# Attention and mixing decoder on one core: the transposed scores six steps behind the row maxima in place of eight

## What is computed

```python
x = x + _L0_attn_ref(_layernorm(x), w_qkv, w_proj)
# in it, for each of 16 sequences b and 16 heads h:
attn = jnp.einsum('bnhd,bmhd->bhnm', q, k) * SCALE
attn = jax.nn.softmax(jnp.where(causal, attn, NEG), axis=-1)
out = jnp.einsum('bhnm,bmhd->bnhd', attn, v)      # then a bit-linear projection
# in the feed-forward network, for gate_w, up_w and down_w:
wq = w.astype(jnp.float8_e4m3fn).astype(x.dtype)
```

## Time and profile before

| | us |
|---|---|
| median of 3 runs (1488.34 to 1490.43) | 1490.22 |
| the profiled execution | 1488.82 |
| its span, first to last instruction | 1487.0 |
| PE, DVE, ACT, POOL busy, of the span | 1390.5, 1234.5, 871.8, 1177.6 |
| time outside the span, in the profiled execution | 1.8 |
| first row scores begin | 48.83 |
| first transposed scores begin | 76.26 |
| attention steady, eight steps | 24.79 |
| last maxima of rows begin | 442.41 |

### The profile page before, as it was taken

The page is one execution under the profiler, slowest core; times in us unless marked ns, Lnnn a source line. Parts: engine busy times, 40 slices in busy tenths (PEclk is TensorE's granted clock), DMA queues, the critical chain, the costliest instruction groups (busy, mean ns, idle before and its releaser), DMA issues.

```text
span 1487.0 us, 23871 instructions
## 1 busy us (share of the span) xinstructions
PE 1390.5 (94%) x8327; PEld 775.5 (52%) x8405; DVE 1234.5 (83%) x1964; ACT 871.8 (59%) x1437; POOL 1177.6 (79%) x902
## 2 busy tenths in 40 slices
PE   3698999999986898899999999999999999999998
PEld 2577787878764443334444444444444444444443
DVE  6789999999984799789898899899889888888611
ACT  5589999999886223444545455455456446544341
POOL 3279999999985687888888878878887888788532
PEclk9799999999998899999999999999999999999999
DMA  5545565655431533222422331332323232240001
GB/s 191 132 111 152 139 167 139 167 139 152 127 83 58 175 100 81 68 50 71 100 50 52 91 78 43 79 78 64 78 64 71 62 81 50 68 102 15 18 19 29
DMA packets 171587, 133.57 MB, mean 90 GB/s; under 512 B 120500, under 2 KB 124748, under 8 KB 171468
## 3 DMA queue, kind: packets, MB, share of 16 engines
q1 hardware_dynamic: 171276, 131.91, 35.4%
q10 hardware_dynamic: 192, 0.14, 0.0%
HBM read 50.67 MB, written 19.92 MB: 47 GB/s over the span
## 4 chain that ended last, share of the span: by engine, by line
PE 64%; DVE 12%; POOL 8%; issue 7%; ACT 7%; DMA 1%; SPq 0%; POOLq 0%; DVEq 0%; ACTq 0%
PE gu L839 20%; PE gu L853 10%; PE shared_bank L784 9%; POOL pL L1782 3%; PE y L806 3%; PE y L800 3%; PE y L803 3%; PE y L808 3%; PE y L809 3%; DVE blockmax L980 2%; DVE o_sb L1020 2%; DVE z L1210 1%; DVE qkt L960 1%; PE s_kq L632 1%; ACT pH L1427 1%
## 5 line engine op out<-in xcount | busy, mean ns | idle before, releaser
L1654 ACT ACTIVATE shared<-shared_bank 128x512 f32<-128x512 f32 x162 | 96.1, 593 | 320.5 <-PE shared_bank L784 320.5
L1207 DVE TENSOR_TENSOR y<-shared,y 128x512 f32<-128x512 f32 x324 | 223.9, 691 | 41.2 <-ACT shared L1654 22.1
L1782 POOL TENSOR_TENSOR pL<-pT,pH 128x768 f16<-128x768 f32 x128 | 217.0, 1698 | 12.9 <-ACT pH L1427 7.4
L839 PE MATMUL gu<-fT,wg 128*128 128x512 f16 x768 | 181.4, 379 | 1.5 <-DMA fT<-fnl 1.5
L1214 DVE TENSOR_REDUCE oT<-z 128x64 f32<-128x512 f32 x256 | 175.6, 686 | 8.7
L839 PE MATMUL gu<-fT,wu 128*128 128x512 f16 x768 | 182.2, 380 | 0.0
L1210 DVE TENSOR_TENSOR z<-y,cT 128x512 f32<-128x512 f32 x236 | 162.3, 688 | 10.7 <-PE y L798 4.4
L1916 POOL TENSOR_TENSOR fuL<-fu,fuH 128x512 f16<-128x512 f32 x96 | 112.0, 1167 | 71.8 <-ACT fuH L1669 71.6
L853 PE MATMUL gu<-wd,fuL 128*128 128x512 f16 x384 | 145.6, 379 | 0.0
L853 PE MATMUL gu<-wd,fuH 128*128 128x512 f16 x384 | 145.6, 379 | 0.0
L1852 POOL TENSOR_TENSOR kv<-vT,cT 128x1024 f32<-128x1024 f32 x70 | 137.8, 1970 | 5.9 <-ACT vT L1609 5.9
(11 more groups left out here) (222 smaller groups left out, 3540.2 us busy)
## 6 DMA issues: line engine op xcount, KB each, us to landing
pack<-qkhl SPq DMA_DIRECT2D x256, 128.0 KB, 2.6
x_sb<-in_x SPq DMA_DIRECT2D x16, 512.0 KB, 4.0
c_sb<-in_ctx SPq DMA_DIRECT2D x32, 256.0 KB, 4.0
hankel<-in_L_xattn_k SPq DMA_DIRECT2D x32, 256.0 KB, 4.1
out_y<-yo SPq DMA_DIRECT2D x32, 256.0 KB, 2.9
x_grp<-x_scratch SPq DMA_DIRECT2D x30, 256.0 KB, 3.5
x_scratch<-x_sb SPq DMA_DIRECT2D x14, 512.0 KB, 3.0
wraw<-in_L_attn_w_qkv SPq DMA_DIRECT2D x3, 1024.0 KB, 9.6
```

The source lines that it names most:

```text
L839: made = T.matmul(bank[:], (wg, wu)[which][:, cb, ib * P:(ib + 1) * P], fT[:, cb, part, :], start=cb == 0 and part == 0, stop=cb == CB - 1 ...
L1207: chain.step(V.tensor_tensor(bank[:], shared[2 * part + half][:], bank[:], op))
L1782: G.tensor_tensor(pL[n % 2][:], pT[n % NP][:], pH[n % NP][:], ALU.subtract).then_inc(low_done, 1)
```

## The change

PROB goes from `HP + 4` = 8 to `HP + 2` = 6. FINISH and the steps of exponentials, parts and weighing hang on it and move up by two as well. NORM_AT, PROJECT_AT and the six places of a weights' piece move up by two. The four operations on the maxima, spread over four steps before (k = 0, 1, 2, 3), now stand in two: joined and turned at k = 0, both parts at k = 1. What is moved in the first steps: the turning of the value and projection weights comes later, `stats_in(2)` and the weights' magnitude ahead of `ternary(2)`. Piece 0 comes seven steps behind its place in place of four.

```diff
-        PROB = HP + 4
+        PROB = HP + 2
...
-        NORM_AT, PROJECT_AT = -2 * PAIRS - 8 - LOAD_AHEAD, -PAIRS - 5
+        NORM_AT, PROJECT_AT = -2 * PAIRS - 10 - LOAD_AHEAD, -PAIRS - 7
...
-        FIRST_V_AT, FIRST_V_SPLIT_AT = (17, 19), (18, 20)
-        V_WEIGHTS_AT, PROJ_WEIGHTS_AT, LOAD_PIECES_AT = (-1, 0), (1, 2), 3
-        OUT_SCALE_AT, OUT_SIGN_AT = -1, 0
+        FIRST_V_AT, FIRST_V_SPLIT_AT = (18, 19), (19, 20)
+        V_WEIGHTS_AT, PROJ_WEIGHTS_AT, LOAD_PIECES_AT = (1, 2), (3, 5), 6
+        OUT_SCALE_AT, OUT_SIGN_AT = -1, 1
...
-        MASK_AT, CLAMP_AT, FACTOR_AT, ADD_AT, TAKE_AT, STORE_AT = 2, 3, 4, 11, 12, 13
+        MASK_AT, CLAMP_AT, FACTOR_AT, ADD_AT, TAKE_AT, STORE_AT = 0, 1, 2, 9, 10, 11
...
-            return n if k == (0 if n else 4) and 0 <= n < PIECES else None
+            return n if k == (0 if n else 7) and 0 <= n < PIECES else None
...
@@ tensor_program: ahead of the output projections, and no longer at the step's end
+                for use, k in halves(t):
+                    if k == 0:
+                        turn_max(use)
...
-                for use, k in halves(t):
-                    if k == 1:
-                        turn_max(use)
...
@@ vector_program
+            stats_in(2)
             magnitude(3, WB, 4)
-            ternary(2)
...
+                for use, k in halves(t):
+                    if k == 0:
+                        join_max(use)
                 for i, blocks in turning(t - 1):
                     copy_weights(i, blocks)
+                if t == OUT_SCALE_AT:
+                    ternary(2)
...
-                    if k == 3:
-                        low_max(use)
...
-                    if k == 0:
-                        join_max(use)
+                    if k == 1:
+                        low_max(use)
...
@@ scalar_program
+                    if k == 1:
+                        high_max(use)
...
-                    if k == 2:
-                        high_max(use)
```

More of the change, by code:

```diff
@@ L327, in project_steps @@
         def project_steps(t):
-            for b, k in batches(t, PROJECT_AT, PAIRS + 13):
+            for b, k in batches(t, PROJECT_AT, PAIRS + 15):
                 if b > 0 or k >= PAIRS:
@@ L1087, in weight_bound @@
             def weight_bound():
+                w.wait_ge(fw_pow_done, PIECES)
                 chain.step(V.tensor_reduce(out=mx[:, 0:2], in_=wmax[:], op=ALU.max, axis=AXIS.X))
@@ L1142, in vector_program @@
                 for b, k in batches(t, NORM_AT, LOAD_AHEAD + 11, 2):
-                    if k == LOAD_AHEAD:
+                    if k == LOAD_AHEAD and b > 2:
                         stats_in(b)
```

## The result

The changed kernel takes 1507.51 us (median of 4 runs, 1504.6 to 1508.22) against 1490.33 (4 runs, 1488.34 to 1490.48): ratio 1.0115, interval 1.0097 to 1.0132. The prediction said slower, 1497, range 1490 to 1501.5. The profiled execution took 1506.81 us, its span is 1505.0, 18.0 more than before. One execution of a later kernel, e5b, ran at a granted clock of 0.61 in place of the usual 0.98 and took 2256.57 us; it is left out of that kernel's median and ratio.

What follows compares the result with a forecast made beforehand. The prediction held POOL, PE and ACT all full in the first stage's middle, with room only in fill and drain. Its terms, 6.7 (fill's gain inside) + 1.3 - 1.9 + 0.8 = +6.9 us on 1490.2, gave 1497, range 1490 to 1501.5.

Steps and rivals of the forecast that it cites:

- Term 2: Steady middle of the first stage: moving the maxima into two steps costs 0 us (-0.5 to +2.6).
- It fits by 0.09: Steady middle: low_max would end at 236.07, before PE takes its bank at 236.16.
- Rival 3: Steady middle: low_max misses PE's bank by 0.2 us in each of 13 sequences, +2.6, 1499.7 us; chance 0.12.
- Term 1: Loop fill: transposed scores 0 stand behind seven row scores, not nine; -4.7 us (-1.9 to -6.5).
- my bound of 6.5: Loop fill: the most that can be gained, two whole steps of 3.25 us each.
- deduction of 1.8 for mask and clamp: Loop fill: piece 0's mask and clamp now come later on DVE, reducing the gain from 6.5 to 4.7 us.
- Term 3: Piece 0: piece 2's mask waits for a load behind pack's 16 issues; +6.7 us (+3.5 to +10), fill gain included.
- term 4: After the wait for the load: PE runs at 1.2 GHz for a step or so, +1.3 us (0 to 2).
- the sum of 5.3: By the skill's rule of small issue time, POOL alone holds the load: piece 0 costs 5.1, the whole change 5.3.
- Term 5: Pairs 11 to 27: POOL has worked off pieces 0 and 1 during the wait, -1.9 us (-2.5 to 0).
- Term 6: Loop drain: the last two row scores share steps with transposed scores 120 and 121, +0.8 us (0 to 1.4).

Runs made afterwards that it cites:

- e5b: Changed kernel with low_max ahead of high part and value splitting on DVE, and high_max first in ACT's step: 1504.1 us, ratio 1.0107.
- e2: Changed kernel with every weights' piece one sequence later, pieces 0 and 1 eight steps apart like the others: 1487.6 us, ratio 0.9991.
- g1: Changed kernel in which POOL starts low_qk, in the step of DVE's L1020, only when L1020 is done: 1499.1 us, ratio 1.0071.
- h2: e2 plus g1's wait of POOL for L1020, nothing else: 1488.1 us, ratio 0.9996.
- i2: h2 with turn_max at the end of PE's step, as in e4: 1486.5 us, ratio 0.9985.
- f1: e2 in which DVE repeats the maxima of pair 16 14 times more, one stop of some 13 to 14 us: 1507.8 us, ratio 1.0122.
- i1: Kernel before the change with every weights' piece one sequence later, as in e2, and weight_bound waiting for all pieces: 1488.2 us, ratio 0.9994.
- e3: Changed kernel with low_max put ahead of high_part in DVE's step, still at k = 1: 1505.9 us, ratio 1.0111.
- e4: Changed kernel with turn_max at the end of PE's step, still at k = 0: 1507.8 us, ratio 1.0123.
- f3: Changed kernel in which POOL makes the low part of pair 56 three times, 3.3 us more, once: 1507.9 us, ratio 1.0126.
- f4: Changed kernel with the fourth pack's 16 transfers behind piece 0's store and piece 2's load on SP: 1503.3 us, ratio 1.0095.
- h1: e2 with low_max ahead of the values on DVE, high_max first on ACT, and g1's wait of POOL: 1488.4 us, ratio 0.9998.

## Why the prediction was wrong

**Term 2, the middle, is the step that failed.** It said 0, at most +2.6, "It fits by 0.09". It came to +9.8 from exponential 19 to 99. Slower was forecast, and the stop made it so; these 9.8 us took the time out of the range. The bank that I weighed was fine: between 192 and 440 us no wait of PE for `low_max` shows. What I never asked is which engine would set the pace once the maxima moved, and where DVE's two operations on SBUF fall beside POOL's. Of the 1.0 us per sequence, 0.3 belongs to the new order itself (25.09 in e2, g1 and h2 against 24.79), and 0.7 to the collision (g1's wait removes it, i2's removes 0.84). That the slow alignment lasts ten sequences is shown (f1). Why it lasts is argued and not shown: the collision makes DVE late, and a late DVE may start L1020 late again. Rival 3 named the place and the sign, but its price, 0.2 us, was that of another mechanism. Of the 0.3, `turn_max` ahead of the values accounts for at most 0.1 (25.00 in i2 against 25.09 in h2), `low_max` was not shown to account for any; the rest stays open.

**Term 1, the fill**: -4.7 was mis-sized. Exponentials 4 to 10 came 5.6 to 7.1 us earlier, and i1 against e2 gives 7.0 with the pieces out of the way, just past my bound of 6.5. Row scores 6, the last that both kernels have ahead of transposed scores 0, begin at the same time; before first, then now:

```profile
68.20 0.39 PE L611 MATMUL s_qk<-pack 128*128 128x256 f16 x2 [1.13 <-DVE blockmax L980]
```
```profile
68.11 0.39 PE L611 MATMUL s_qk<-pack 128*128 128x256 f16 x2 [0.37 <-DVE blockmax L980]
69.06 0.42 PE L632 MATMUL s_kq<-pack 128*128 128x128 f16 x2 [0.22 <-issue]
```

The two steps taken away lasted 74.80 - 68.20 = 6.6 us, and they came off whole, waits included; the way from the last row scores to the transposed scores is 0.5 us shorter as well (0.95 against 1.46). What failed is the deduction of 1.8 for mask and clamp: at exponential 4 the lead was down to 5.6, but at 10 it was 7.06 again. Where those steps won it back stays open.

**Terms 3 and 4, the stop**, were right in mechanism and nearly in size, in part by luck: exponential 11 was forecast at 118.6 and measured at 119.17, but at 115.8 to 117.3 in the profiles of e3, e4, e5b, f3 and g1, which have the same stop. Errors also cancelled. The forecast had `pack` at 97.8 (102.5 - 4.7), 11.5 us of issues and 3.4 from load to mask; `pack` began at 96.84, took 12.09, and load to mask took 5.1. Term 3 came to 114.69 - 106.47 = 8.2 in place of 6.7. From the mask's start to exponential 11 it was 4.48 us against 4.13 before, so term 4 came to 0.35 in place of 1.3; the mask itself was 0.68 us shorter, which hid the rest, 1.0. PE came out of the stop at the lower clock, 1.2 GHz: granted clock 0.50 in the window from 116 to 119 us, and 0.61 us for row scores that take 0.38 in the steady part:

```profile
116.00:119.00 3.00, 2.82 (x18) 2.18 (x19) 2.90 (x7) 0.00 (x0) 0.00 (x0) 0.50 0.17 69
```
```profile
116.18 0.61 PE L611 MATMUL s_qk<-pack 128*128 128x256 f16 x2 [14.43 <-DVE blockmax L980]
...
241.69 0.38 PE L611 MATMUL s_qk<-pack 128*128 128x256 f16 x2
```

The row of 12.09 us of issues, and the 1.7 to 3.5 us that f4's order gives back, bear out the sum with the issues in it. A single issue is 12.09 / 16 = 0.76 us, where such a transfer lands 2.7 us after its issue (median); it is the sixteen in a row that the store and the load stand behind. The Trainium skill, "DMA: Bandwidth & Descriptors", section "Issuing engines are not separate DMA queues", calls the time to initiate a transfer usually small beside the transfer; these rows show 0.76 us beside 2.7 for one, and the sum of 5.3 that I drew from the sentence was wrong for sixteen.

**Term 5**: -1.9 forecast up to exponential 27. Measured -1.9 up to exponential 19 (8.57 to 6.68), and -1.4 up to 27 (7.19), where the slow rise has begun. **Term 6, the drain**: +0.8 forecast, +0.86 measured between exponentials 119 and 127.

With term 2 at 9.8 in place of 0, the forecast's 6.9 becomes 16.7; measured 17.2 between the medians.

## What to carry to other kernels

Where a stage has every engine near full, a period read from one trace is a property of the order and of the alignment in which it happened to run; a change that stops the loop once can leave it in another. Before costing a steady stage at nothing, list the VectorE operations with two SBUF inputs and what GpSimd runs beside them, and ask what a shift of half a microsecond does to who comes second. And when such a collision shows, an added wait on the engine with slack can be the cheapest cure.

## What the hardware showed that I had not expected

- L1020, 128x1024 from two SBUF inputs, takes 1.22 us alone (h1), 1.31 to 1.67 when it starts in the last 0.6 us of a POOL operation, 1.88 to 2.19 when it starts 0.06 to 0.35 us into one. POOL's operation that starts behind it goes from 1.16 to 2.15 or from 1.65 to 2.63 us.
- The same steady program ran at 25.09 us per sequence (e2) and at 25.8 (f1) for about ten sequences each, by what one stop near pair 11 had left behind.
- The 16 issues of `pack` held SP's queue for some 10.2 to 13.0 us wherever they stood in one row, so what stands behind them in program order is late by that.
